# A two-block transformer kernel with a selective scan: projection and convolution of the later batches moved into the first scan, by way of DRAM

## The reference, cut to what matters

```python
x = einsum('bld,ed->bel', hidden_states, in_proj_w)          # 256 -> 512 channels
xc = conv_general_dilated(x, conv_w, ..., feature_group_count=d_inner)   # 4 taps per channel, causal
x = silu(xc + conv_b[None, :, None])
x_dbl = einsum('bdl,ed->bel', x, x_proj_w)                   # low rank dt, B, C
dt = softplus(einsum('brl,dr->bdl', dt_low, dt_proj_w) + dt_proj_b[None, :, None])
# for each of 16 states n:  h = h * exp(dt * A[:, n]) + (dt * x) * B[n];  y += h * C[n]
y = (y + D * x) * silu(z)                                    # z = layernorm of the block's input
```

## Time and profile before

| | |
|---|---|
| three runs | 955.51, 957.46, 957.96 us; median 957.46 |
| profiled execution | 957.83 us, of it 956.0 us span |
| granted PE clock, mean over the span | 0.934 |
| PE busy | 808.4 us, 85% |
| DVE busy | 781.4 us, 82% |
| ACT busy | 654.5 us, 68% |
| POOL busy | 521.1 us, 55% |
| DMA | 119.55 MB, mean 125 GB/s |

### The profile page before, as it was taken

The page is one execution under the profiler, slowest core; times in us unless marked ns, Lnnn a source line. Parts: engine busy times, 40 slices in busy tenths (PEclk is TensorE's granted clock), DMA queues, the critical chain, the costliest instruction groups (busy, mean ns, idle before and its releaser), DMA issues. The chain is left out here.

```text
span 956.0 us, 9316 instructions
## 1 busy us (share of the span) xinstructions
PE 808.4 (85%) x2770; PEld 403.2 (42%) x2810; DVE 781.4 (82%) x905; ACT 654.5 (68%) x988; POOL 521.1 (55%) x445
## 2 busy tenths in 40 slices
PE   6621247799799999999799999998899999898999
PEld 2210123354344344454344444444344444447887
DVE  4699997895999998986999998978999998853333
ACT  4899979674688963775789863775789864623442
POOL 0688786312899884203998882216998871022000
PEclk9855558899999999999999999999999999999999
DMA  8179982001299965301599962301799961201321
GB/s 302 35 136 219 279 188 47 1 1 45 56 202 237 232 137 149 110 2 44 106 218 235 233 138 83 111 1 44 160 226 215 213 149 50 89 0 45 98 101 66
DMA packets 46817, 119.55 MB, mean 125 GB/s; under 512 B 5792, under 2 KB 6944, under 8 KB 46256
## 3 DMA queue, kind: packets, MB, share of 16 engines
q0 software_dynamic: 16128, 58.73, 33.2%
q1 hardware_dynamic: 30640, 60.24, 18.4%
HBM read 56.03 MB, written 4.19 MB: 63 GB/s over the span
## 5 line engine op out<-in xcount | busy, mean ns | idle before, releaser
L1682 POOL TENSOR_TENSOR work<-du,bcast 128x1024 f32<-128x1024 f32 x128 | 349.8, 2762 | 32.6 <-ACT bcast L874 32.3
L1289 DVE TENSOR_TENSOR_SCAN pair<-pair,work 128x512 f32<-128x512 f32 x256 | 299.2, 1214 | 17.9 <-POOL work L1682 11.1
L889 ACT ACTIVATE pair<-dt,a_neg 128x512 f32<-128x512 f32 x256 | 165.8, 681 | 36.9 <-DVE work L1296 34.0
L660 PE MATMUL bank<-stage,ring 128*128 128x512 f32 x384 | 174.3, 597 | 9.6 <-ACT bcast L874 8.1
L1296 DVE TENSOR_TENSOR work<-pair,ccast 128x1024 f32<-128x1024 f32 x128 | 156.8, 1225 | 11.6
L1697 POOL DMA_DIRECT2D u<-work x112 | 118.9, 1062 | 37.1 <-DVE work L1296 12.6
L660 PEld LDWEIGHTS bank<-stage,ring 128*128 128x128 f32 x384 | 72.8, 191 | 81.6 <-issue 74.4
L441 PE MATMUL bank<-xd,pick 128*128 128x512 bf16 x108 | 46.9, 434 | 68.7 <-ACT bcast L874 39.8
L1668 POOL TENSOR_SCALAR fst<-fst 128x1 f32<-128x1 f32 x32 | 9.2, 288 | 164.6 <-DVE fst L1523 164.3
L674 PE MATMUL bank<-ring,stage 128*128 128x512 f32 x192 | 85.6, 594 | 1.7 <-ACT hx L1167 1.7
L441 PEld LDWEIGHTS bank<-xd,pick 128*128 128x128 bf16 x128 | 12.9, 101 | 127.8 <-ACT bcast L874 68.0
(11 more groups left out here) (169 smaller groups left out, 1476.2 us busy)
## 6 DMA issues: line engine op xcount, KB each, us to landing
u<-work POOLq DMA_DIRECT2D x112, 512.0 KB, 5.8
ring<-ffn_dram SPq DMA_DIRECT2D x120, 256.0 KB, 4.8
ring<-ffn_dram SPq DMA_DIRECT2D x16, 512.0 KB, 3.3
xres<-x_dram SPq DMA_DIRECT2D x4, 1024.0 KB, 5.2
stage<-w_dram SPq DMA_DIRECT2D x1, 4096.0 KB, 17.1
stage<-w_dram SPq DMA_DIRECT2D x4, 1024.0 KB, 7.6
out_dram<-stage SPq DMA_DIRECT2D x16, 256.0 KB, 2.1
ctxT<-ctxT_dram SPq DMA_DIRECT2D x4, 512.0 KB, 8.2
```

Source lines behind the costliest of these rows:

```text
L660: last = pe.matmul(banks[UP_BANKS[f % 3]][:], piece(b, f)[:, k * P:(k + 1) * P], xnT[:, k, :], start=k == 0, stop=k == J - 1)
L889: act.activation(pairs[s % DECAYBUFS][:, q, :], dt[:, p * HALF + q, :], ACT.Exp, scale=a_neg[:, p * HALF + q, n:n + 1]).then_inc(s_decay, 1)
L1289: dve.tensor_tensor_scan(pair[:, q, :], pair[:, q, :], rows[:, q, :], 0.0, ALU.mult, ALU.add).then_inc(s_scan, 1)
L1682: pool.tensor_tensor(work[:, s % SCANBUFS, :, :], du[:, p * HALF:(p + 1) * HALF, :], bcast[:, n % 2, :].unsqueeze(1).broadcast_to([P, HALF ...
```

## The change

**Moved.** The projection and the convolution of batches 2, 1 and 3 (in this order; twelve channel groups) are made in the first scan. PE projects a group into bank 2, ACT copies it to `rows_in` (in `hx`), PE convolves it with four matmuls whose weights are diagonal matrices `taps` (in `ring`, made by POOL at the start from `ident` and the taps), ACT writes it with its bias to `rows_out` (in `hT`), and SP stores it to an internal DRAM tensor. Project of group a stands at one half-step, its convolution at the next, its write-out at the one after. `load_u` brings a batch's 1 MB back into `u` when the batch before has left it. The batches' `between` loses `project`, `project_copy` and `convolve`.

**Reordered.** The lists of `between` on PE, ACT and DVE are new; so are parts of the weight quantisation, POOL's order of the norms, and SP's list.

```diff
-W_MEAN = {6: 0, 10: 1}
+W_MEAN = {6: 0, 12: 1}
...
-W_LATE = (("scale", 1, 2), ("sign", 1, 2), ("scale", 1, 3), ("sign", 1, 3))
+W_LATE = (("scale", 1, 0), ("sign", 1, 0), ("scale", 1, 1), ("sign", 1, 1), ("scale", 1, 2), ("sign", 1, 2))
+W_LAST = (("scale", 1, 3), ("sign", 1, 3))
+AHEAD_BATCHES = (2, 1, 3)
+MEAN_AFTER = 2
+AHEADS = len(AHEAD_BATCHES) * J
+AHEAD_AT = {3 + 9 * g + 2 * j: J * g + j for g in range(len(AHEAD_BATCHES)) for j in range(J)}
...
+            def load_u(b):
+
+                sp.wait_ge(s_yT, (b - 1) * T + T)
...
+                sp.dma_start(u[:], ahead_d[b - 1].rearrange("(j p) l -> p j l", p=P)).then_inc(s_uload, 16)
...
+            def ahead_project(a):
...
+                if a:
+                    pe.wait_ge(s_arows, a)
...
+                for k in range(KC):
+                    last = pe.matmul(banks[2][:], ipw[:, k, j * P:(j + 1) * P], rows[:, k, :],
+                                     start=k == 0, stop=k == KC - 1)
+                last.then_inc(s_aproj, 1)
+
+            def ahead_convolve(a):
+
+                j = a % J
+                pe.wait_ge(s_arows, a + 1)
...
+                for k in range(TAPS):
+                    last = pe.matmul(banks[3][:], taps[:, j, k, :], rows_in[:, a % 2, k:k + L],
+                                     start=k == 0, stop=k == TAPS - 1)
+                last.then_inc(s_aconv, 1)
...
+            def ahead_copy(a):
+
+                act.wait_ge(s_aproj, a + 1)
+                if a >= 2:
+                    act.wait_ge(s_aconv, a - 1)
+                act.activation(rows_in[:, a % 2, PAD:], banks[2][:], ACT.Copy).then_inc(s_arows, 1)
+
+            def ahead_out(a):
+
+                g, j = divmod(a, J)
+                act.wait_ge(s_aconv, a + 1)
+                if g:
+                    act.wait_ge(s_astored[j], g * 16)
+                act.activation(rows_out[:, j, :], banks[3][:], ACT.Identity,
+                               bias=pch[:, j, PC_CONVB:PC_CONVB + 1]).then_inc(s_aout, 1)
...
             def silu_u(b):
-                act.wait_ge(s_conv, b * J + J)
+                act.wait_ge(s_uload, b * 16)
...
                 if not rest:
                     for step in W_LATE:
                         weight(*step)
                 turning(m)
+                if not rest:
+                    for step in W_LAST:
+                        weight(*step)
...
                 h_quant(b, 0)
-                convolve(m, 0)
-                convolve(m, 1)
+                h_scale(b, 2)
                 h_quant(b, 1)
-                convolve(m, 2)
-                convolve(m, 3)
...
             pool.wait_ge(s_const, const_wait)
+            pool.wait_ge(s_first, first_wait)
+            for j in range(J):
+                for k in range(TAPS):
+                    pool.tensor_scalar(taps[:, j, k, :], ident[:], pch[:, j, k:k + 1], 1.0, ALU.mult,
+                                       ALU.mult).then_inc(s_taps, 1)
```

More of the change, by code:

```diff
@@ L832, in pass_ @@
                     attention(m, prev, slot, 1, 0)
+                    if not rest:
+                        ahead(slot, 1, 0)
                     if rest:
@@ L836, in pass_ @@
                     attention(m, prev, slot, 1, 1)
+                    if not rest:
+                        ahead(slot, 1, 1)
                     if rest:
```

201 lines of the change are left out of this document (138 added, 63 removed).

## The result

| | before | after |
|---|---|---|
| median of 8 runs of each, us | 957.68 (955.51 to 959.82) | 965.36 (959.99 to 971.01) |
| ratio, with its 95% interval | | 1.0084 [1.0049, 1.0118] |
| profiled run, us: whole, span | 957.8, 956.0 | 967.69, 965.9 |
| mean granted clock of the profiled run | 0.934 | 0.956 |

The forecast was 944 us and faster. The changed kernel is 0.8% slower. First, where the time went. "After" is the changed kernel, "later `between`" the second and third.

What follows compares the result with a forecast made beforehand. Later passes were taken to hang on PE in `between` and DVE in the scan; the first scan on DVE and ACT. 957.8 - 2 x 6.6 - 3.0 + 2.2 = 943.8 us, forecast 944, range 939 to 949.

Steps and rivals of the forecast that it cites:

- Taken out of each `between`: Later `between`: PE loses 7.3 us of projection, waits about 1.3 in new places; 6.6 us gained each, bounds 5.2 and 8.0.
- a PE without a pause is the state in which the clock stood at 1.0 everywhere else: First scan: reason to stay near the low end of bounds 0 to +55 us, since PE at 1.2 GHz would have no pause.
- Rival 1: First scan: clock goes up and down, each convolution 5.7 us in place of 3.65; 10 us more, 954; chance 0.20.
- The two `norm_apply` 0.9: End of later `between`: both follow POOL's two products and take 0.9 us; second half-step near 454.9 in place of 461.5.
- 5.2 us sooner: End of later `between`: first half-step 5.2 us sooner, not 6.0, as copy, table load and half a decay follow the last `attend`.
- The first scan, +2.2: First scan ends 2.2 us later: DVE loses 4.7, 3.70 of waiting for POOL absorbed, 2 for one clock drop; bounds 0, +55.
- The first turning, +2.7: First turning: second weight mean in the last slot makes the first `q_scale` 3.9 us later, of which 2.7 reach PE.
- The load of `u`: `between`: 1 MB load on SP's queue lands at 400.8, ahead of the Silu at about 405.8; hidden with 5 us of cover.
- Rival 2: First scan: DMAs collide, with 3 MB of stores and 1 MB of loads more; +6.8 us, 951; chance 0.09.
- rival 3: First scan: PE stays at 1.2 GHz through all twelve pairs, 5 us a pair; +55 us, about 997; chance 0.05.
- Slower: Whole kernel: slower by more than 0.3% (2.9 us), from rival 3 and the upper end of Rival 1; chance 0.09.
- Rival 4: `between` hangs on new waits (late load of `u`, GELU ahead of quantisation): 3 us instead of 6.6 each, 951; chance 0.09.

Runs made afterwards that it cites:

- run 5: Changed kernel with the four step-size matmuls contracting over 128 rows in place of 16 (added rows zeros): median 954.8 us, ratio 0.9959.
- Run 7: Changed kernel with DVE's `norm_apply(6)` moved to the end of `between`, ahead of the first half-step: median 949.1 us, ratio 0.9881.
- the seven: Profiles of the changed kernel and six edited ones, with first scan and turning as in after: first scan 123.8 to 128.8 us, `h_scale(0)` at 191.2 to 195.9.
- run 4: Changed kernel with one tap of four in the twelve moved convolutions, so it computes something else: median 960.5 us, ratio 1.0030.
- run 11: Changed kernel with four filler matmuls in each half-step of states 1 to 8 of the first scan without a moved convolution: median 959.9 us, ratio 1.0015.
- run 1: Changed kernel with 24 of the 16 + 40 filler matmuls left, in one piece behind the last attention transposes: median 964.3 us, ratio 1.0051.
- run 9: Changed kernel with 128 rows for the step-size matmuls and `norm_apply(6)` ahead of the first half-step: median 939.9 us, ratio 0.9785.
- run 10: Kernel before with 128 rows for the step-size matmuls and `norm_apply(6)` ahead of the first half-step: median 953.9 us, ratio 0.9948.
- Run 2: Changed kernel with PE's third norm transpose put back behind `down1(3)` in the later batches, as in the kernel before: median 963.6 us, ratio 1.0066.
- run 3: Changed kernel with the later batches' first C broadcast ahead of the last `attend`, as in the kernel before: median 962.5 us, ratio 1.0035.
- run 14: Changed kernel with 128 step-size rows, early `norm_apply(6)`, 24 turning fillers, split convolutions, first-scan fillers, and POOL's second-mean root ahead of its last sums: 934.3 us, ratio 0.9755.
- run 15: Kernel of run 14 with both last norms' roots ahead of POOL's second state product and both `norm_apply` ahead of the first half-step: 940.6 us, ratio 0.9814.

## Why the prediction was wrong, by its own steps

**"Taken out of each `between`", 7.3 us of projection and the new waits.** Right, but at a clock that I took from the kernel before. I followed the new list "with each instruction's duration in that `between`"; up to the step sizes it ran as walked: the second pass starts 9.7 us late (its first `h_scale` at 403.65 and not 393.98), and the Silu that I had at about 405.8 begins with its table load at 415.33. Then the clock fell for some 6 us, in a PE without a pause: 3.6 us a pass (run 5). The sentence that failed is "a PE without a pause is the state in which the clock stood at 1.0 everywhere else". It even had a case against it: in the first `between` of before the clock fell right behind the same four matmuls (0.74 from 221 to 226 us), and I booked that as not of the change's making, half of it as going away. Rival 1 put the clock's trouble into the first scan alone. The profiles show the granted share of the clock and no frequency: what the prediction calls 1.2 and 2.4 GHz is a granted clock of 0.50 and 1.00, at which 512 columns took 0.427 and 0.216 us, 1.20 and 2.37 columns a ns.

**"The two `norm_apply` 0.9".** The step that failed second. I let them follow POOL's two products, as in the earlier trace rows. In after the products ended at 465.9, and 0.6 us later POOL had the next product, and the bias behind it; the second `norm_apply` missed the gap. Predicted for the second half-step: 6.6 us sooner; measured 0.6 with the turning before it. Run 7 gives 4.4 us a pass by moving one instruction. With both losses taken away the stage is 8.6 us shorter than before, above my 6.6 and 0.6 beyond its bound of 8.0.

**The first half-step, "5.2 us sooner".** Measured 3.2. The wait for ACT's chain behind the last `attend` (1.2 us on DVE) came as walked: start at 458.3, copy, table load, decay. But 5.2 was itself too small: with the clock kept up (run 5) the first half-step comes 6.8 us sooner (53.8 us behind the first `h_scale`, before 60.6), so the clock took 3.6 and not 2.0. Two errors of opposite sign stand in this term.

**The first scan, +2.2.** Measured 6.2 in this profile, 1.9 to 6.9 in the seven. The terms as written, 4.7 less 3.70 and 2 for the clock, make 3.0 and not 2.2. The absorption was right (no wait of DVE for POOL was left), the waits of ACT for PE were not: I had allowed one slow convolution, there are three (5.40, 6.38 and 5.40 us, at 78.23, 91.17 and 109.75). At the second of them the decay that DVE wants is held up further by the weight step next in ACT's list. Rival 1 named the slow convolutions and priced them at 12 x 1.4, from 5.7 us for one that starts at 0.50, an estimate that stands in no row; here it came with three of twelve, and ACT waited 8.3 us in five places (7.0 + 1.3). The medians of runs 4 and 11 are 5 us below after, the landmark `h_scale(0)` 3.6 and 0.4.

**The first turning, +2.7.** Measured 3.2; the two later ones, 0, are unchanged at 23.6. This term held, in part by luck. POOL's root took 4.2 us (165.27 to 169.45) and not 2, but POOL's own sums ended 1.8 us earlier against DVE's last sums than in the kernel before, and the three pairs took 12.1 us and not 12.6 (six times the 2.0 that I wrote would be 12.0). What the reading of the new list had left out are the fillers ahead of the mean, instructions of PE that compute nothing: without them the turning would have had its old length (run 1, 23.7 us), so the cost that I priced was for the most part not needed.

**The load of `u`, rivals 2 and 3.** Hidden as forecast: ACT's table load ahead of the Silu, at 415.33, waits for nothing. Rival 2 (the DMAs) is not seen in any wait on DVE; rival 3 did not come. "Slower" had a chance of 0.09, from rival 3 and the upper end of rival 1, and came for the most part by two mechanisms that no rival named. Rival 4 had the outcome, a `between` that gives little, by other waits.

**In sum.** Of the 23.9 us between the sum of 943.8 and the profiled 967.7: 12.0 in the second and third `between`, settled by runs 5, 7, 9 and 10; 5.2 in the first, where the same two edits give 7.6 (run 9); 0.5 in the first turning; 4.0 in the first scan, where run 4 shows that the length of the convolutions matters, but no run how much of it is the clock. The opening, the later scans and the closing make 2.2 more, in code that the change left alone but for the taps.

Open: why the kernel before, with the same 16-row matmuls between the same neighbours, kept its clock in two of three passes. Run 2 restored those neighbours and it fell in two of three. Also why the clock, kept up in `between`, falls at the scan's start instead.

## What to carry to other kernels

A walk through a new order needs the granted clock in it, and DVE's delays beside POOL, not only durations: ask of each stretch of PE without pause whether what it runs is narrow (behind 16 rows 0.50 was granted here), and of each short DVE instruction whether POOL stands in front (0.52 us became up to 4.6). A loss that one pass of the old kernel shows and the others don't is a warning about the margin of all of them. An untouched stretch that varies by 5 us from profile to profile can't price an edit of that size by one profile; several kernels that share the stretch give the range to hold it against. And when a change disappoints, look for two instructions before blaming the idea: here a padded weight and one moved normalisation turned 0.8% slower into 2.2% faster than the kernel before, which the same two edits make 0.5% faster.

## What the runs showed of the hardware

- A PE that was busy 6.00 of 6.00 us was granted 0.50 (after, 438 to 444 us). Four matmuls of 16 rows (435.35 to 440.02 us, with transposes on both sides) lead into it; with 128 rows and all else equal the window of run 5 reads 1.00 (433 to 439 us). Slow `down1(3)`: 23 of 27 passes with 16 rows in the new order, 0 of 18 with 128.
- Not every pass was hit, and unchanged code was too: of the three passes of before one was, of those of runs 1 to 4 two each.
- A 0.52 us instruction of DVE took from 0.86 to 4.6 us beside POOL's products of 2.3 us, and ended each time 0.28 to 0.30 us behind the end of a POOL instruction, in seventeen profiles. Moved to where DVE was idle it gave 4.4 us, over eight times its length.
- The root of the weight mean, four POOL instructions on one column, took 2.0 us in the five profiles where it ends by the start of DVE's last sums, or 0.1 us behind it (before and runs 1, 10, 14 and 15), and 3.9 to 5.2 us in the twelve where it stands beside them. What it is that slows it no run here parts.
- Scatter is smaller in the kernels without these losses, though they were run less often: the kernel with both edits lies within 936.6 to 941.7 (four runs), run 14 within 933.6 to 935.4 (four), after within 960.0 to 971.0 (eight).
